# A transformer row kernel: 38 idle products of two columns ahead of TensorE's program in place of 6 of 128 columns

## Chip, cores and metric

The kernel runs on one core of a Trainium2 chip. The metric is the device time of one execution in microseconds, lower is better.

## The reference, cut to what matters

For each of 16 rows (batch entries) of 512 tokens by 512 features, in float32: a layer norm without gain or bias, `xn`; multi-head attention on `xn` with 16 heads of 32, causal mask, biases; a gated feed-forward on the same `xn`, with weights of -1, 0 or 1, 1408 wide, and scales per channel; the output is the sum of both and of the input.

```python
xn = _layernorm(x, axis=-1)
# attention
qkv = jnp.einsum('bsd,ed->bse', xn, w_qkv) + b_qkv
scores = jnp.einsum('bhqd,bhkd->bhqk', q, k) / math.sqrt(32) + causal
out = jnp.einsum('bhqk,bhkd->bhqd', softmax(scores), v) @ w_out.T + b_out
# feed-forward
g = (xn @ gate_w.T) * gate_s
u = (xn @ up_w.T) * up_s
ffn = ((silu(g) * u) @ down_w.T) * down_s
x + out + ffn
```

## The kernel before, in words

All large operands are split into two float16 parts, high and low, and a product in float32 precision is made of three float16 products (high by high, low by high, high by low). All weights stay in the core's memory for the whole run. Each engine has its own program, written out by hand, and they meet through semaphores alone.

**TensorE's program** (line 517 on) has four parts. First a lead-in: it waits for the constants (line 665), makes the idle products of `PE_PAD` (lines 666 to 668), turns the first maxima of the weights with `turn_max(0)` (line 669, defined at 643), spreads the scale with `spread(0)`, waits for the turned first row and computes q, k and v of row 0 (lines 672 to 683). Then `period(0, "first")`, a loop over rows 1 to 14 (lines 742 and 743), `period(B - 1, "last")` and `period(B, "tail")`. `period` has 20 slots. In every even slot it makes the scores of one unit of four heads (`scores`, line 605), in each slot a hand-written share (`PLAN`, line 66) of the products for q, k, v, gate, up, down and the output projection (`fill`, line 688), and the products of P by V of the slot two back (`values`, line 622), for which P has been turned by a DMA transpose that SP issues (lines 506 and 508). Every product goes through `mm` (line 519), so most of TensorE's work has line 520 in the profile. Products that write 512 columns take the bulk of the time; those of `values` write 68 or 34, those of the scores 128 to 512 on a quarter of the rows.

**The idle products** write `turned_max`, two partitions by 128 columns of bank 4, from the constants `ones` and `identity`. Nothing reads what they write: `turn_max(0)` starts the same place afresh. `turn_max(0)` waits for `qkv_batch`, which DVE raises once it has the maximum magnitude of the qkv weights in `amax` (line 959).

The hint at the loop's head is number 2,257, the branch back number 4,569, so the body has 2,313. It includes 26 short stretches under `pe.If` (lines 552 and 570), for low halves of the feed-forward weights; with weights of -1, 0 and 1 all low halves are zero, and these products are skipped.

**What orders the rest.** DVE takes the maxima of the scores and reads out results; ACT exponentiates and rounds to the high parts; POOL subtracts to get the low parts (line 1244 for P), normalises the next row (`normalise`, line 1220); SP issues every DMA in order: the transposes of P (lines 506, 508), of the next row's x (`turn_x`, line 439) in slot 15, of the attention output (`turn_o`, line 455), and loads and stores.

Of the kernel before, what the change touches and what calls it, by code (L numbers as in the profile page):

```python
# [40 lines left out]
CB = CW // P  # L41
LAG_V = 2

PE_PAD = 6

def regions(unit):
# [212 lines left out]
def block_program(nc, x, w_qkv, gate, up, w_out, down, smalls, b_out, down_s, out):  # L260
    with ExitStack() as ctx:
        def sb(name, shape, dt=F32):
            return ctx.enter_context(nc.sbuf_tensor(name, shape, dt))
# [29 lines left out]
        identity = sb("identity", [P, P])  # L293
        ones = sb("ones", [P, P])
# [38 lines left out]
        turned_max = ps[0:2, 4, 0:P]  # L333
# [184 lines left out]
        def _(pe):  # L518
# [145 lines left out]

            pe.wait_ge(consts_done, N_CONSTS)
            for _ in range(PE_PAD):
                nc.tensor.matmul(turned_max, lhsT=ones[:, 0:2], rhs=identity[:, :], start=True, stop=True,
                                 skip_group_check=True)
            turn_max(0)
            spread(0)  # L670
# [654 lines left out]
```

## Time and profile before

| | us |
|---|---|
| median of 3 runs | 1992.68 (1989.34 to 1994.12) |
| the profiled execution: its own time | 1988.57 |
| its span, first to last instruction | 1986.8 |
| matmuls busy (PE) | 1895.1, 95% of the span |
| weight loads busy (PEld) | 912.0, 46% |
| VectorE (DVE) | 1347.7, 68% |
| ScalarE (ACT) | 1295.6, 65% |
| GpSimd (POOL) | 1362.8, 69% |
| mean granted clock of TensorE | 0.989 of full speed |

Times are in microseconds from the start of the span unless marked ns. PE is TensorE's matmuls, PEld its weight loads, PEldq its sequencer's own instructions (branches, register work), DVE is VectorE, ACT ScalarE, POOL GpSimd, SP SyncE. A row names line, engine, operation, what is written and read, with shapes and count. Idle time of an engine is put down to what ended it; "issue" means that nothing the profile shows was waited for. A "busy" matmul isn't an array at its peak, since the ends are modelled. Queue 8 of the DMA listing, "instruction", carries program code.

### The profile page before, as it was taken

To read this page: it belongs to the slowest core of one execution; us is meant where nothing else is said; L and a number is where in the kernel's file an instruction comes from. 1 tells how busy PE (TensorE), PEld (TensorE's weight loads), DVE (VectorE), ACT (ScalarE), POOL (GpSimd) and SP (SyncE) were. 2 spreads that over 40 slices of the span, in tenths; PEclk is the share of its full clock that TensorE was granted. 3 is DMA by queue.
4 is the path that set the end of the run, shared out by engine and by line. 5 is a ranking of instruction groups with operands and counts; after the bars stand their busy time and mean duration, and the time that the engine had idled before them with its cause. 6 is when DMAs were issued, how large, how long until landed. Compare 5 with 4: busy or idle time off the path is not lost.

```text
span 1986.8 us, 48299 instructions
## 1 busy us (share of the span) xinstructions
PE 1895.1 (95%) x15560; PEld 912.0 (46%) x15560; DVE 1347.7 (68%) x3925; ACT 1295.6 (65%) x2315; POOL 1362.8 (69%) x1097
## 2 busy tenths in 40 slices
PE   5879999999999999999999999999999999999995
PEld 2334444444444444444444444444444444444442
DVE  7895666757667675666767566676766767666663
ACT  4776766766667666666766666676666766666662
POOL 1285786766768676686866768676676866768764
PEclk9889999999999999999999999999999999999998
DMA  9148768596776868768586776859677686876855
GB/s 333 38 83 152 145 112 153 106 158 133 120 144 120 144 128 149 144 113 154 104 157 128 139 147 110 151 112 157 138 121 144 116 148 128 149 144 114 154 86 117
DMA packets 840049, 267.89 MB, mean 135 GB/s; under 512 B 812864, under 2 KB 812864, under 8 KB 839232
## 3 DMA queue, kind: packets, MB, share of 16 engines
q1 hardware_dynamic: 839872, 265.15, 70.6%
q8 instruction: 158, 2.59, 0.6%
q14 instruction: 19, 0.16, 0.0%
HBM read 46.94 MB, written 16.78 MB: 32 GB/s over the span
## 4 chain that ended last, share of the span: by engine, by line
PE 59%; POOL 14%; issue 8%; DVE 7%; SPq 6%; DMA 4%; ACT 1%; DVEq 0%; POOLq 0%; ACTq 0%
PE ps L520 59%; POOL phl L1244 6%; SPq L442 4%; POOL region_b L1222 3%; DMA p_t<-phl 3%; POOL memory L1239 2%; DVE p L1155 2%; DVE memory L938 1%; SPq L508 1%; POOL region_a L1227 1%; SPq L506 1%; POOL rstd L1218 1%; DVE hidden_tmp L1069 1%; POOL o_hl L1249 1%; DVE hidden_tmp L1075 1%
## 5 line engine op out<-in xcount | busy, mean ns | idle before, releaser
L520 PE MATMUL ps<-x_t,memory 128*128 128x512 f16 x4384 | 1003.0, 381 | 16.3 <-DMA x_t<-region_a 6.7
L1244 POOL TENSOR_TENSOR phl<-p,phl 128x1024 f16<-128x1024 f32 x320 | 683.4, 2136 | 478.0 <-ACT phl L865 478.0
L855 ACT ACTIVATE p<-p,nmax 128x384 f32<-128x384 f32 (+3 forms) x1024 | 530.0, 557 | 288.3 <-DVE nmax L1155 268.9
L520 PEld LDWEIGHTS ps<-x_t,memory 128*128 128x128 f16 x4384 | 406.5, 98 | 513.7 <-issue 56.0
L1155 DVE CUSTOM_DVE_ANT_0 p<-ps,causal,cst 128x384 f32<-128x384 f32 (+3 forms) x1024 | 515.5, 547 | 98.3 <-PE ps L520 85.0
L865 ACT CAST phl<-p 128x1024 f16<-128x1024 f32 x320 | 334.1, 1044 | 52.4 <-DMA p_t<-phl 36.9
L520 PE MATMUL ps<-memory 128*128 128x512 f16 x1408 | 322.6, 379 | 0.8 <-DVE bout_bc L1007 0.8
L1239 POOL TENSOR_TENSOR memory<-hidden_tmp,memory 128x512 f16<-128x512 f32 x176 | 204.0, 1159 | 69.4 <-ACT memory L827 69.4
L1163 DVE TENSOR_REDUCE ps<-ps 128x132 f32<-128x264 f32 (+1 forms) x320 | 122.1, 381 | 184.3 <-PE ps L520 184.0
L520 PEld LDWEIGHTS ps<-vv,p_t 128*128 128x128 f16 x5120 | 187.3, 96 | 94.8 <-issue 21.3
L520 PE MATMUL ps<-vv,p_t 128*128 128x68 f16 (+1 forms) x5120 | 193.5, 185 | 16.1 <-DMA p_t<-phl 15.9
L520 PEld LDWEIGHTS ps<-memory 128*128 128x128 f16 x1408 | 131.4, 98 | 154.7 <-issue 6.6
L873 ACT CAST o_hl<-o 128x128 f16<-128x128 f32 (+1 forms) x320 | 87.8, 274 | 160.8 <-DVE o L1173 160.1
L520 PE MATMUL ps<-memory,region_a 128*128 128x512 f16 x768 | 175.3, 382 | 10.4 <-DMA region_a<-o_hl 10.4
L1069 DVE SCALAR_TENSOR_TENSOR hidden_tmp<-hidden_tmp,ps 128x512 f32<-128x512 f32 x176 | 120.1, 682 | 87.0 <-ACT hidden_tmp L820 86.5
L520 PE MATMUL ps<-memory,x_t 128*128 128x512 f16 x768 | 173.3, 379 | 0.0
L1025 DVE SCALAR_TENSOR_TENSOR qk<-ps,smalls_in,qk 128x512 f16<-128x512 f32 x128 | 96.0, 750 | 95.0 <-ACT qk L764 95.0
L820 ACT ACTIVATE hidden_tmp<-ps,tanh_scale 128x512 f32<-128x512 f32 x176 | 119.5, 679 | 51.8 <-PE ps L520 46.5
L520 PE MATMUL ps<-qk 32*128 32x128 f16 (+3 forms) x3072 | 135.8, 301 | 14.1 <-issue 9.1
L764 ACT ACTIVATE qk<-ps,smalls_in 128x512 f16<-128x512 f32 x128 | 87.3, 682 | 80.9 <-PE ps L520 79.1
L1249 POOL TENSOR_TENSOR o_hl<-o,o_hl 128x128 f16<-128x128 f32 (+1 forms) x320 | 126.1, 394 | 9.2 <-ACT o_hl L873 9.2
L1075 DVE SCALAR_TENSOR_TENSOR hidden_tmp<-hidden_tmp,h_scale,ps 128x512 f32<-128x512 f32 x176 | 130.8, 743 | 2.1
(78 smaller groups left out, 1320.1 us busy)
## 6 DMA issues: line engine op xcount, KB each, us to landing
region_b<-x SPq DMA_DIRECT2D x32, 1024.0 KB, 5.6
out<-region_b SPq DMA_DIRECT2D x64, 256.0 KB, 2.7
p_t<-phl SPq DMA_TRANSPOSE x640, 3.1
memory<-w_qkv SPq DMA_DIRECT2D x3, 1024.0 KB, 8.8
memory<-down SPq DMA_DIRECT2D x1, 2816.0 KB, 21.3
memory<-gate SPq DMA_DIRECT2D x1, 2560.0 KB, 9.5
memory<-up SPq DMA_DIRECT2D x1, 2560.0 KB, 15.3
x_t<-region_a SPq DMA_TRANSPOSE x64, 3.4
```

Of the source, the lines that this page charges most:

```text
L520: return nc.tensor.matmul(o, lhsT=l, rhs=r, start=start, stop=stop, skip_group_check=True)
L820: nc.scalar.activation(hidden_tmp[:, f % 2, :], ps[:, bank, :], ACT.Tanh, scale=tanh_scale[:, f:f + 1]).then_inc(sem["tanh_done"], 1)
L855: last = nc.scalar.activation(cols, cols, ACT.Exp, scale=-1.0, bias=nmax[:, s % 2, i:i + 1])
L865: nc.scalar.copy(phl[:, s % 2, 0, :], p32[:, s % 2, :]).then_inc(sem["p_hi"], 1)
L1025: v.scalar_tensor_tensor(out=qk[:, t, side, 1, :], in0=ps[:, bank, :], scalar=bqkv[:, tile:tile + 1], in1=qk[:, t, side, 0, :], op0=ALU.ad ...
L1069: v.scalar_tensor_tensor(out=hidden_tmp[:, f % 2, :], in0=hidden_tmp[:, f % 2, :], scalar=1.0, in1=ps[:, bank, :], op0=ALU.add, op1=ALU.mu ...
L1075: v.scalar_tensor_tensor(out=hidden_tmp[:, f % 2, :], in0=hidden_tmp[:, f % 2, :], scalar=h_scale[:, f:f + 1], in1=ps[:, bank, :], op0=ALU ...
L1155: v.tensor_tensor_reduce(p32[:, s % 2, col:col + w], ps[:, 2 * (s % 2) + jj, col - 512 * jj:col - 512 * jj + w], causal[:, S - w:S], cst[: ...
L1163: v.tensor_reduce(o_sums(n), o_halves(n), AX, ALU.add).then_inc(sem["o_sum"], 1)
L1239: g.tensor_tensor(h_t(1, f), hidden_tmp[:, f % 2, :], h_t(0, f), ALU.subtract)\
L1244: g.tensor_tensor(phl[:, s % 2, 1, :], p32[:, s % 2, :], phl[:, s % 2, 0, :], ALU.subtract)\
L1249: g.tensor_tensor(o_dst(s, 1), o_src(s), o_dst(s, 0), ALU.subtract).then_inc(sem["o_lo"], 1)
```

## The change

It raises the number of idle products in TensorE's lead-in from 6 to 38 and makes each write two columns instead of 128. They stand ahead of all else in TensorE's program, so everything behind them, the row loop included, moves back by the instructions added.

```diff
-PE_PAD = 6
+PE_PAD = 38
...
             pe.wait_ge(consts_done, N_CONSTS)
             for _ in range(PE_PAD):
-                nc.tensor.matmul(turned_max, lhsT=ones[:, 0:2], rhs=identity[:, :], start=True, stop=True,
+                nc.tensor.matmul(turned_max[:, 0:2], lhsT=ones[:, 0:2], rhs=identity[:, 0:2], start=True, stop=True,
                                  skip_group_check=True)
             turn_max(0)
             spread(0)
```

## Rows read from the trace of the kernel before

**Rows 1.** The page: busy times of the span, and the code's DMA queue.

```profile
PE 1895.1 (95%) x15560; PEld 912.0 (46%) x15560; DVE 1347.7 (68%) x3925; ACT 1295.6 (65%) x2315; POOL 1362.8 (69%) x1097
...
q8 instruction: 158, 2.59, 0.6%
```

**Rows 2.** Busy time in one iteration: length, then PE, PEld, DVE, ACT, POOL.

```profile
543.39:661.75 118.36, 116.61 (x968) 56.20 (x969) 79.74 (x241) 78.61 (x142) 85.45 (x69) 1.00 0.72 135
```

**Rows 3.** Waits of TensorE, whole span: us in total, times, longest.

```profile
PE ps L520 <- issue: 9.5, 14, 1.1
```

**Rows 4.** Waits of TensorE from 424.3 to 543.4, the same columns.

```profile
PE ps L520 <- DMA x_t<-region_a: 1.1, 1, 1.1
PE ps L520 <- DMA p_t<-phl: 0.5, 1, 0.5
```

**Rows 5.** Timeline of TensorE, first products of iterations: start, us, [idle before].

```profile
305.71 0.61 PE L520 MATMUL ps<-qk 32*128 32x512 f16 x8 [0.70 <-issue]
...
543.39 0.83 PE L520 MATMUL ps<-qk 32*128 32x512 f16 x12 [0.81 <-issue]
...
897.29 0.83 PE L520 MATMUL ps<-qk 32*128 32x512 f16 x12 [0.26 <-issue]
...
1723.70 0.83 PE L520 MATMUL ps<-qk 32*128 32x512 f16 x12 [0.50 <-issue]
```

**Rows 6.** Line 742, the loop: ns min/median/max, first and last start.

```profile
L742 PEldq COMPARE_BRANCH  x14: 85/1256/1624, 304.1 to 1839.6; - x14
```

**Rows 7.** The same line in two windows, around 541.7 and around 896.1.

```profile
L742 PEldq COMPARE_BRANCH  x1: 1304/1304/1304, 541.7 to 541.7; - x1
...
L742 PEldq COMPARE_BRANCH  x1: 806/806/806, 896.1 to 896.1; - x1
```

**Rows 8.** Timeline of TensorE where the loop is left.

```profile
1839.96 0.60 PE L520 MATMUL ps<-vv,p_t 128*128 128x68 f16 x16
1840.49 0.83 PE L520 MATMUL ps<-qk 32*128 32x512 f16 x12
```

**Rows 9.** DMA queues, 661.75 to 780.00, one iteration: packets, MB, share.

```profile
q8 instruction: 10, 0.16, 0.6%
```

**Rows 10.** DMA queues, in turn 540:541, 541:544, 544:545, 894:895.

```profile
q8 instruction: 1, 0.02, 6.0%
...
q1 hardware_dynamic: 1594, 0.40, 124.4%
...
q8 instruction: 1, 0.02, 5.5%
...
q8 instruction: 1, 0.02, 7.3%
```

**Rows 11.** Timeline of TensorE ahead of and behind one back edge.

```profile
534.18 2.76 PE L520 MATMUL ps<-x_t,memory 128*128 128x512 f16 x12
...
537.64 0.60 PE L520 MATMUL ps<-vv,p_t 128*128 128x68 f16 x16
538.09 4.04 PE L520 MATMUL ps<-memory 128*128 128x512 f16 x18
541.98 0.60 PE L520 MATMUL ps<-vv,p_t 128*128 128x68 f16 x16
...
548.06 3.18 PE L520 MATMUL ps<-memory,x_t 128*128 128x512 f16 x14
```

**Rows 12.** Timeline of TensorE, the idle products.

```profile
3.50 2.72 PE L667 MATMUL ps<-identity,ones 128*2 128x128 f32 x12 [3.50 <-POOL identity L1213]
```

**Rows 13.** The chain that ended last, its pieces on TensorE in one iteration.

```profile
543.39 61.48 PE ps L520 x508
...
660.67 1.08 issue
```

**Rows 14.** Timeline of TensorE, turn_max(0).

```profile
20.29 0.58 PE L646 MATMUL ps<-identity,amax 128*2 128x128 f32 x2 [14.07 <-DVE amax L959]
```

**Rows 15.** Timeline of TensorE, the first products of row 0.

```profile
26.62 6.74 PE L520 MATMUL ps<-x_t,memory 128*128 128x512 f16 x24 [4.19 <-DVE memory L938]
```

## The prediction, made before the changed kernel was run

> **What bounds the kernel now.** The page first: TensorE's array is busy for 95% of the span, the next engine for 69% [rows 1]. Within the steady row loop it is tighter: 116.61 of 118.36 us in one iteration [rows 2]. Whatever lets TensorE stand still there costs time, unless something else would have held it anyway. The whole idle time of the array, by what ended it, is short. Its one entry with no releaser is "issue", 9.5 us in 14 places [rows 3]; of the others, what recurs in the loop is a wait for turned x and one for turned P, 1.1 and 0.5 us in the iteration to 543.4 [rows 4].
>
> The timeline shows where those are. Thirteen stand before the first score products of an iteration, 0.26 to 1.08 us each, for example 0.81 before 543.39 and 0.26 before 897.29 [rows 5]; read at all thirteen back edges, from 305.71 to 1723.70, they add up to 9.11 us (the rest of the 9.5 is elsewhere). The line of the loop shows the cause: its closing COMPARE_BRANCH takes 1256 ns in the median [rows 6]. The same instruction took 1304 ns ahead of the idle 0.81 and 806 ahead of 0.26 [rows 5, 7]: the idle time is the branch less some 0.5 us that products already queued cover. The last of the loop's 14 branches, which leaves the loop and goes straight on, took 85 ns, the shortest of the fourteen [rows 6], and the array ran on without a gap from 1839.96 to 1840.49 [rows 8]. So what costs is going back, not the instruction.
>
> Why going back costs is read from the instruction queue. It moved 158 packets, 2.59 MB, or 16.4 KB each [rows 1]; an instruction of the compiled program has 64 bytes, so a packet is a block of 256. The loop body has 2,313 instructions, 9.04 blocks, and an iteration fetches ten [rows 9]: the body isn't kept, every block is fetched again, one at a time. Around the branch at 541.66 to 542.97 there is a packet in 540 to 541, none in 541 to 544 (that window has the data queue's alone), one in 544 to 545 [rows 10]. I read this as follows: on entering a block TensorE's sequencer asks for the next one, and in the block that holds the branch the hint at the loop's head makes that the head's block. The packet of 540 to 541 is the head's; the branch waits until it can be used; on landing the next block is asked for, and its packet follows 1.0 to 2.0 us after 542.97. The fetch is thus asked for 1.0 to 2.0 us before its packet and usable 2.0 to 3.0 us after that starts: 3.0 to 5.0 us in all, I take 4.
>
> How late the request is: 1.0 to 2.0 us ahead of 540 to 541 is 538.0 to 540.0, or 1.7 to 3.7 us before the branch. Products of 512 columns follow each other there at 0.22 us, two instructions each [rows 11], so the block with the branch is entered 16 to 34 instructions before it. Too late for a fetch of 4 us: 4 less 2.7 is the 1.3 us of the branch.
>
> **The change, part by part.**
> (a) Place. The six idle products are 12 weight loads and 12 matmuls in the records [rows 12], two of each per product. 32 more are 4 x 32 = 128 instructions, exactly half a block, ahead of everything. All block borders move back by 128 in the program. The branch then stands 144 to 162 instructions into its block, the head 136 to 154 (it is always 8 less, 2,312 being 9 x 256 + 8), and 154 + 2,313 = 2,467 is under 2,560: still ten blocks.
> (b) The branch. The head's block is asked for 128 instructions, some 61 products, earlier. Counting back from the branch: the 9 or so short products that remain of the sixteen, 18 long ones, 16 short, and 18 long of the stretch before (4, 12 and 2 more), from about 534 on: some 7 us earlier [rows 11]. With the 1.7 to 3.7 us of before the lead is about 9 us against at most 5.0 needed. The branch no longer waits for code, and the 0.5 us of queued products covers what is left of it (85 ns on leaving). Gain: the thirteen idles, 9.11 us. At the exit the next products even overlapped by 0.07 us (1839.96 + 0.60 against 1840.49) [rows 8], 13 x 0.07 = 0.9 more. Between 9.1 and 10.0 I take **9.5 us**.
> (c) Does it reach the end? The chain of one iteration runs from the products at 543.39 for 61.48 us, then over DVE to the normalisation of the next row, POOL's queue and SP's transposes back to the products of the last slots, and ends in 1.08 us of issue, the back edge itself [rows 13]. Array and chain both begin behind the edge, so each edge shortens the cycle by its own idle; the waits for x and P [rows 4] neither grow nor shrink. The bound from below is that half is swallowed, a gain of 4.6, where those transfers turn out to hang on something else; above, 10.0.
> (d) The new landing. From the head only 256 less 136 to 154, 102 to 120 instructions, are left to the next block, not some 240. It is asked for on landing, usable within 5.0 us. The timeline has 12, 16 and 16 products from the head to 548.06 [rows 5, 11], so the block begins 4 to 13 products after that, and the array needs it no earlier than 548.9 - 543.4 = 5.5 us after its first product. Cost 0; where the fetch took 2 us longer it would be 1 us an iteration at most.
> (e) The idle products themselves. Six of 128 columns took from 3.50 to 6.22 us, 2.72 for 12 records, about 0.21 apart [rows 12]. 76 at that pace, longer than two-column ones should need, end at 3.5 + 16.2 = 19.7 us. TensorE has nothing to do until DVE has the maxima of amax, which release turn_max(0) at 20.29 after 14.07 us of rest [rows 14]. Cost 0; the cover is 0.6 us, and past it each further 0.1 us would be paid once. They write only what turn_max(0) rewrites. A warmer array later is bounded by the first 24 products, 6.74 us against 24 x 0.22 = 5.3, a gain of at most 1.4 [rows 15]; with 6 us of rest still between, I take 0.
> (f) The exit. There the hint fetches a block that isn't used, and the one after it was only fetched some 5 us later. It is needed 128 instructions earlier now. Between 0 and one fetch, 5 us, once; the queue of products (the sequencer ran well over 16 products ahead) covers it, 0.
> No semaphore, DMA or other engine's instruction changes.
>
> Sum: 0 - 9.5 + 0 = -9.5 us on the profiled execution of 1988.57, giving 1979.1. That execution lies 4.1 under the median of the runs, 1992.68; on the median it is 1983.2.
>
> **Rivals.**
> R1, the place doesn't matter. The branch is taken to code that was last used ten blocks ago, so it fetches on demand wherever it stands, and the idle stays: 1992.7, within 0.3%. Against it: the packet comes before the branch, and the later the branch follows its packet the shorter it is (1304 ns with its packet 0.7 to 1.7 us ahead of 541.7, 806 with one of 894 to 895, 1.1 to 2.1 ahead of 896.1) [rows 7, 10]. The Trainium skill states such a rule (Runtime: NRT & Kernel Launch, Instruction fetch mechanics: a taken branch whose target isn't in the current two-page window forces a fetch before execution goes on); by it the 9.5 would be 0. The trace agrees that taken branches back cost 1256 ns and the fall-through 85, and doesn't show whether a hint is exempt. Chance 0.10.
> R2, the idle goes and comes back as waits for turned x or turned P, wholly or by half: a gain of 0 to 5 us, 1988 to 1993. For it: both waits are there in every iteration; against it: the chain crosses the edge. Chance 0.10.
> R3, slower. What made the exit's next packet so late may be a second request at mid-block, 128 instructions in. The branch now stands 16 to 34 behind that point, where it stood as far behind the border. Then the block after the loop is fetched just before going back, and if it takes the place of the head's block, or goes ahead of the one the landing needs, the branch waits for a whole fetch: 3.0 to 5.0 us, less 0.5 covered, against 0.70 now, so 1.8 to 3.8 more at 13 edges, 23 to 49 us: about 2029. It decides where only two blocks are held at a time. Against it: no eleventh packet is seen in an iteration. Chance 0.12.
>
> **How the numbers follow.** My case has 0.68, R1 and R2 0.10 each, R3 0.12. The measurement tells 0.3%, 6 us, from no change; my case gives 9.5, which clears that by 3.5, as much as runs differ. R2 and part of its neighbours stay under it. So faster 0.67, same 0.20, slower 0.13. The range leaves out R3 and the far end below: from 1979 (12 us gain with a low median, runs spread by 5) to 1993.5 (no gain). My case alone: 1979 to 1987.
>
> **What would show it.** Right: the loop's COMPARE_BRANCH under 400 ns at all 14, "issue" near 0 in the array's waits, ten instruction packets an iteration still, iterations of about 117.4 us, the turn of maxima still at 20.29. Wrong: branch as long as before with its packet still just ahead (the border isn't where I place it), branch longer or eleven packets (R3), branch short but the waits for x and P grown by the same 0.7 (R2), or the first products later than 26.62 (the idle products stick out).

## The result, and the profile after

The changed kernel takes 1970.1 us in the median (1969.0 to 1970.5, 4 runs) against 1992.1 us for the kernel before (1989.3 to 1994.1, 4 runs): a ratio of 0.9893, 95% interval 0.9878 to 0.9908. It is faster by 22 us, where 9.5 were forecast. The profiled executions are 1970.23 and 1988.57, 18.3 apart; the kernel before's lies some 4 us under its own median.

The page of the changed kernel: busy times, the code's queue, and the chain that ended last by engine.

```profile
span 1968.5 us, 48427 instructions
PE 1894.2 (96%) x15624; PEld 913.2 (46%) x15624; DVE 1347.6 (68%) x3925; ACT 1294.5 (66%) x2315; POOL 1361.9 (69%) x1097
...
q8 instruction: 158, 2.59, 0.6%
...
PE 80%; DVE 5%; POOL 5%; issue 4%; SPq 3%; DMA 2%; ACT 1%; DVEq 0%; POOLq 0%; ACTq 0%
```

The engines do the same work as in [rows 1], apart from the 64 records of the 32 added idle products. The chain that ended last now lies on TensorE for 80%, against 59% on the page of the kernel before. What the back edge costs is in the line of the loop and in the timeline around one edge (start, us, idle before):

```profile
L742 PEldq COMPARE_BRANCH  x14: 85/358/381, 304.9 to 1819.8; - x14
```

```profile
305.26 0.60 PE L520 MATMUL ps<-vv,p_t 128*128 128x68 f16 x16
305.80 0.83 PE L520 MATMUL ps<-qk 32*128 32x512 f16 x12
```

The branch fell from 1256 ns in the median [rows 6] to 358, and going back now looks like leaving the loop did in [rows 8]: the next products follow 0.06 us inside the modelled end of the last. The stretch from 304 to 1840 us holds 13 edges in either kernel. TensorE's waits in it, before:

```profile
PE ps L520 <- issue: 9.1, 13, 1.1
PE ps L520 <- DMA x_t<-region_a: 6.2, 10, 1.2
PE ps L520 <- DMA p_t<-phl: 4.4, 11, 0.5
```

and in the changed kernel, the whole answer:

```profile
PE ps L520 <- DMA p_t<-phl: 1.8, 5, 0.7
```

So 9.1 us of issue went, as forecast, and with them 8.8 of the 10.6 us of waits for turned x and turned P, which had been forecast to stay. Iterations are 116.2 to 117.1 us from edge to edge, against 117.3 to 119.1 before. Most of them have nothing left but products. Busy times of one iteration (length, then PE, PEld, DVE, ACT, POOL), to be held against [rows 2], and its instruction queue, as [rows 9]:

```profile
538.40:654.60 116.20, 116.20 (x974) 56.39 (x971) 79.51 (x239) 78.51 (x143) 85.11 (x69) 1.00 0.74 138
```

```profile
q8 instruction: 10, 0.16, 0.5%
```

The lead-in, in TensorE's timeline, against [rows 12, 14, 15]:

```profile
3.50 2.04 PE L667 MATMUL ps<-identity,ones 128*2 128x2 f32 x76 [3.50 <-POOL identity L1213]
20.66 0.59 PE L646 MATMUL ps<-identity,amax 128*2 128x128 f32 x2 [15.12 <-DVE amax L959]
...
27.00 8.02 PE L520 MATMUL ps<-x_t,memory 128*128 128x512 f16 x24 [4.20 <-DVE memory L938]
```

The 76 records take 2.04 us in all. The first products of row 0 begin 0.4 us later and take 1.3 us longer than before; both differ from kernel to kernel, one profiled execution each (26.62 to 27.12 and 6.62 to 8.02 among the kernels below, with no order by the number of idle products).

The account of the profiled pair goes by three stretches, cut at the first and the last start of the loop's branch. The lead-in got 0.8 us longer (304.1 to 304.9). The loop got 20.6 us shorter (1535.5 to 1514.9): 9.1 of issue, 13 x 0.06 of overlap at the edges and 8.8 of waits are 18.7 of it, and 1.9 stay unaccounted for. What comes behind the loop got 1.5 us longer (147.2 to 148.7). Together that is the 18.3.

### The profile page after: what moved, and what is told of

The parts are those of the page before. It is cut to its first block, busy times and chain, and to the rows that moved or that the text cites. A ratio compares the mean times of both kernels' runs of the same rounds, so it can differ in the third digit from the quotient of the medians.

```text
span 1968.5 us, 48427 instructions
## 1 busy us (share of the span) xinstructions
PE 1894.2 (96%) x15624; PEld 913.2 (46%) x15624; DVE 1347.6 (68%) x3925; ACT 1294.5 (66%) x2315; POOL 1361.9 (69%) x1097
## 4 chain that ended last, share of the span: by engine, by line
PE 80%; DVE 5%; POOL 5%; issue 4%; SPq 3%; DMA 2%; ACT 1%; DVEq 0%; POOLq 0%; ACTq 0%
PE ps L520 80%; POOL phl L1244 2%; DMA p_t<-phl 2%; SPq L442 1%; POOL region_b L1222 1%; DVE memory L938 1%; DVE p L1155 1%; POOL memory L1239 1%; SPq L506 1%; SPq L508 0%; POOL region_a L1227 0%; DVE hidden_tmp L1069 0%; SPq L456 0%; POOL rstd L1218 0%; DVE hidden_tmp L1075 0%
## 5 line engine op out<-in xcount | busy, mean ns | idle before, releaser
L820 ACT ACTIVATE hidden_tmp<-ps,tanh_scale 128x512 f32<-128x512 f32 x176 | 119.4, 679 | 51.3 <-PE ps L520 46.1
```

Of the source, the lines that this page charges most:

```text
L820: nc.scalar.activation(hidden_tmp[:, f % 2, :], ps[:, bank, :], ACT.Tanh, scale=tanh_scale[:, f:f + 1]).then_inc(sem["tanh_done"], 1)
```

## Experiments

Two explanations of the 8.8 us stood against each other. **S**: the stall at the edge itself delays the chain to x and P, more than the array. **P**: the change moved not only the branch but all ten code packets of an iteration, by half a block, and two of them had met SP's transposes ahead of x and P. All kernels were timed against the kernel before, taken again each time. The table has every one; shift is the number of instructions by which the loop stands later than in the kernel before, and the last two columns are TensorE's waits from 304 to 1840 us of the profiled execution.

| kernel | shift | ratio to before | issue, us | x and P, us |
|---|---|---|---|---|
| before | 0 | 1 | 9.1 | 10.6 |
| changed | 128 | 0.9893 | 0 | 1.8 |
| pad70 | 256 | 1.0000 (0.9991 to 1.0010) | 10.9 | 11.9 |
| pad2 | -16 | 0.9960 (0.9946 to 0.9975) | 15.5 | 0.9 |
| pad10 | 16 | 0.9996 (0.9987 to 1.0006) | 9.9 | 6.6 |
| pad14 | 32 | 0.9909 (0.9892 to 0.9925) | 0.2 | 4.3 |
| pad22 | 64 | 0.9913 (0.9897 to 0.9930) | 0 | 5.0 |
| pad30 | 96 | 0.9930 (0.9913 to 0.9946) | 0 | 8.9 |
| wide38 | 128 | 0.9884 (0.9868 to 0.9901) | 0 | 1.4 |
| pad46 | 160 | 0.9884 (0.9867 to 0.9900) | 0 | 3.2 |
| pad54 | 192 | 0.9929 (0.9912 to 0.9945) | 0.4 | 6.4 |
| nohint | 128 | 1.0175 (1.0158 to 1.0192) | 41.8 | 1.4 |
| skip_near | 0 | 0.9993 (0.9983 to 1.0002) | 9.4 | 11.3 |
| skip_far | 0 | 0.9948 (0.9932 to 0.9965) | 9.1 | 1.4 |

### Place or products: pad70

```diff
-PE_PAD = 38
+PE_PAD = 70
```

> 70 idle products of two columns: 256 instructions more than the kernel before, so the row loop stands at the same place within its block of 256, while more idle products are run than in the changed kernel. If only the place counts (both theories), this is the kernel before again: the closing branch at 1.0 to 1.6 us, issue idle of 9 us and waits for turned x and P of about 10 us in the loop, total 1990 to 1994. If the idle products themselves do something (for the array's state or the start), it is near 1970.

Measured 1991.4 us against 1991.2. A whole block further on, with 64 more idle products than it, the kernel is the kernel before again, branch and waits for x and P (11.9 us against 10.6, each in one execution) alike:

```profile
L742 PEldq COMPARE_BRANCH  x14: 85/1331/1721, 308.5 to 1847.5; - x14
```

So the idle products act through the place of what follows them, and through nothing else that these runs can tell (the interval is 0.1% wide on either side).

### Their width: wide38

The kernel before with `PE_PAD = 38`, products 128 columns wide.

> 38 idle products as in the changed kernel, but 128 columns wide as before: the same place of the loop, more work ahead of it. By the pace of 0.21 us for a pair of records they end at 19.7 us, ahead of turn_max(0) at 20.3, so the width is worth nothing: the same time as the changed kernel, 1969 to 1972. If the idle products' own work delays the start, it is longer by what they stick out.

Measured 1968.6 us, ratio 0.9884, the same as the changed kernel within the intervals. The products ended even earlier than bounded, 13.3 instead of 19.7 us:

```profile
3.51 9.81 PE L667 MATMUL ps<-identity,ones 128*2 128x128 f32 x76 [3.51 <-POOL identity L1213]
20.72 0.59 PE L646 MATMUL ps<-identity,amax 128*2 128x128 f32 x2 [7.40 <-DVE amax L959]
```

### Without the hint: nohint

```diff
-            with nc.Fori(1, B - 1, engines=type(mybir.ALL_ENGINES)([pe.engine]), hint_back_edge=True) as b:
+            with nc.Fori(1, B - 1, engines=type(mybir.ALL_ENGINES)([pe.engine]), hint_back_edge=False) as b:
```

> The changed kernel with hint_back_edge off in TensorE's loop alone: the branch must fetch its target on demand, about 3.5 to 4 us, idle some 3 us at each of 13 edges, 40 us in all, while the ten packets of an iteration keep their places apart from the one at the edge. Theory P: the waits for x and P stay near the 2 us of the changed kernel, total 2007 to 2012. Theory S: they come back at 10 us or more, total 2018 or more. If the hint has no effect (the rule that a taken branch fetches anyway), it is 1970.

Measured 2026.4 us, ratio 1.0175. The line of the loop, and the waits from 304 to 1840:

```profile
L742 PEldq COMPARE_BRANCH  x14: 76/3827/4107, 303.9 to 1877.3; - x14
```

```profile
PE ps L520 <- issue: 41.8, 13, 3.5
PE ps L520 <- DMA p_t<-phl: 1.4, 4, 0.6
```

The rival R1 falls: the hint does exempt the branch, which without it takes 3827 ns, the whole fetch (I had worked out 3.0 to 5.0). The packets say the same. Without the hint a packet still comes 5.9 to 7.3 us ahead of the branch, and an eleventh, which the changed kernel does without, starts 1.0 to 1.7 us behind the branch's own start. From the start of the packet that it waits for to its end the branch takes 2.3 to 2.9 us here, and 2.4 to 2.7 us at the thirteen edges of the kernel before: the same wait for the head's block, begun at different times.

And S loses its first test, though the total of 2026.4 us lies in the range that it was given (2018 or more): there are 3.2 us of stall at every edge, and no wait for x at all. Against P's range (2007 to 2012) the total is some 14 us too high, for a reason that neither theory had. Behind the long idle the granted clock fell to its lower level, 1.2 GHz, for a while. The timeline behind the first edge, and the window of it (the column before the last two is the granted clock):

```profile
308.25 1.47 PE L520 MATMUL ps<-qk 32*128 32x512 f16 x12 [3.47 <-issue]
309.64 5.74 PE L520 MATMUL ps<-memory,x_t 128*128 128x512 f16 x16
```

```profile
308.25:315.00 6.75, 6.75 (x27) 2.31 (x28) 1.43 (x4) 2.88 (x4) 1.65 (x1) 0.58 0.99 216
```

Twelve score products took 1.47 us where the changed kernel has 0.83, and the next sixteen 5.74, against 3.63 for sixteen at full clock. The clock fell behind nine of the thirteen edges, not behind the fifth to the eighth, though the idle there was as long (3.1 to 3.4 us):

```profile
796.00:803.00 7.00, 6.46 (x53) 3.10 (x54) 2.82 (x8) 2.92 (x4) 2.12 (x2) 1.00 0.84 159
```

The four iterations behind those edges took 119.4 to 119.9 us, which is the changed kernel's 116.5 and the 3.2 of stall; the others took 120.9 to 122.6. So the excess goes with the clock. Why it fell at some edges and not at others isn't shown.

### The packets moved, the edge left alone: skip_far and skip_near

Both are the kernel before, with two stretches in the loop body that never run. They stand behind a branch on the flag that is zero for these weights, 127 and 129 instructions long with it, 256 together. So the branch back stands as late in its block as before, and it takes as long (1156 and 1264 ns in the median of its thirteen jumps back, 1269 before). In skip_far they open slots 11 and 19, in skip_near slots 3 and 5; between the two the packets come half a block elsewhere.

```diff
+                def passed_over(n):
+                    with pe.If(has_lo["gate, up"] != 0):
+                        for _ in range(n):
+                            mm(ps[0:2, 4, 0:2], vv[:, 0, 0, 0:2], vv[:, 0, 0, 0:2], True, True)
+
                 for s in range(NCH if cur else TAIL_SLOTS):
+                    if mode == "mid" and s in (11, 19):
+                        passed_over({11: 63, 19: 64}[s])
```

> The kernel before, with two stretches of products in the loop body that are never run (passed over by a branch on the zero flag), 127 and 129 instructions long, at the start of slots 11 and 19. The branch back stands as late in its block as before (256 instructions more in the body), but between slots 11 and 19 the code packets come half a block elsewhere, away from the two places where they met SP's transposes before turned x and P. Theory P (packets meeting SP's transposes make x and P late): issue idle stays at 9 to 11 us, waits for x and P fall from 10.6 to 5 us or less, total 1983 to 1986. Theory S (the stall at the edge brings them on): all stays, 1991, or more for the eleventh packet.

> The same two passed-over stretches, but at the start of slots 3 and 5, so that only the packets of slots 3 and 4 move and those of the second half of an iteration lie where they lay in the kernel before. Both theories: the kernel before again, issue idle 9 to 11 us, waits for x and P about 10 us, total 1990 to 1994. If the stretches themselves cost something, it shows here and is to be taken off skip_far.

Measured: skip_far 1979.6 us against 1990.7, 11.1 faster; skip_near 1989.9 against the same, no difference that can be told. The waits, first of skip_far, then of skip_near:

```profile
PE ps L520 <- issue: 9.1, 13, 1.1
PE ps L520 <- DMA p_t<-phl: 1.4, 3, 0.6
```

```profile
PE ps L520 <- issue: 9.4, 13, 1.1
PE ps L520 <- DMA x_t<-region_a: 6.5, 10, 1.2
PE ps L520 <- DMA p_t<-phl: 4.8, 12, 0.5
```

This settles it between the two. With the same stall at the edge, and with the same two stretches to pass over, the waits for x and P are there or not by where the packets of the second half of an iteration fall: P holds, S falls. The total was expected at 1983 to 1986 and is lower, since nearly all of the 10.6 us went and not half. How a packet makes x and P late is seen on SP. The kernel before in one iteration (start, us), the instruction queue from 526.0 to 527.2, and the landing of the last of the four transposes of x, issued at 524.7 (min/median/max of that one):

```profile
517.54 2.52 SPq L508 DMA_TRANSPOSE p_t<-phl  x1
520.40 5.53 SPq L442 DMA_TRANSPOSE x_t<-region_a  x4
526.19 2.29 SPq L506 DMA_TRANSPOSE p_t<-phl  x1
528.59 1.24 SPq L508 DMA_TRANSPOSE p_t<-phl  x1
```

```profile
q8 instruction: 1, 0.02, 7.2%
```

```profile
DMA to landing us min/median/max: 4.9/4.9/4.9
```

The same of skip_far, where the last transpose of x is issued at 642.1; from 642 to 649 its DMA has the data queue alone and no code packet:

```profile
637.77 5.69 SPq L442 DMA_TRANSPOSE x_t<-region_a  x4
643.71 1.23 SPq L506 DMA_TRANSPOSE p_t<-phl  x1
645.06 1.27 SPq L508 DMA_TRANSPOSE p_t<-phl  x1
```

```profile
q1 hardware_dynamic: 5133, 1.28, 109.8%
```

```profile
DMA to landing us min/median/max: 3.5/3.5/3.5
```

A transpose takes SP 1.23 us to issue; these, where a code packet comes with it, 2.3 to 2.6 (that of 517.54, 93 us behind the head of 424.29, met the packet before, which falls between 518 and 519). And the last transpose of x, in flight when the packet comes, lands after 4.9 us instead of 3.4 or 3.5. Read over the whole loop of the kernel before, the 13 transposes of x that had a packet start between the end of their issue and their landing landed after 4.6 to 5.4 us, the other 39 after 3.3 to 4.2. The issue is less regular: of the 107 transposes that had a packet start between 0.6 us ahead of their own start and 0.9 us behind it, half took over 1.8 us and some the usual 1.23, and one transpose of P in every iteration took 2.4 to 3.4 us some 7 us behind the head, with no packet there. How a packet holds them up inside the DMA isn't shown. The one delay holds the products that need x (they began at 529.59, 524.7 + 4.9, after 1.15 us of waiting), the other the P of slot 15 behind it, which the products of slot 17 read, 0.52 us more. In skip_near the packet is back at this spot, and so is the slow issue:

```profile
644.70 1.23 SPq L506 DMA_TRANSPOSE p_t<-phl  x1
646.05 2.60 SPq L508 DMA_TRANSPOSE p_t<-phl  x1
```

The changed kernel has no packet there: its P transposes behind x take 1.23 and 1.26 us, and the last transpose of x, issued at 522.1, landed after 3.4. It has one earlier, within the four for x, which take 6.46 us together instead of 5.53 and still land in time.

```profile
516.90 6.46 SPq L442 DMA_TRANSPOSE x_t<-region_a  x4
523.61 1.23 SPq L506 DMA_TRANSPOSE p_t<-phl  x1
524.96 1.26 SPq L508 DMA_TRANSPOSE p_t<-phl  x1
```

### Other places: shifts of -16 to 192

Each is the changed kernel with another `PE_PAD`: 2, 10, 14, 22, 30, 46, 54.

> 10 idle products of two columns: the loop moves by 16 instructions only, so the head's block is asked for about 1.7 us earlier than in the kernel before, and the closing branch should take 0.4 us or less with no issue idle. The packets of code otherwise stay within about 2 us of where they were. Theory P (packets of code that fall on SP's transposes make turned x and P late, apart from the branch): the waits for x and P stay near 8 to 10 us in the loop, total about 1981 to 1984. Theory S (the stall at the edge itself brings those waits on): they go with it, total about 1970 to 1973.

Measured 1989.9 us: not as either theory said. The shift of 16 didn't free the branch (median 1342 ns, issue 9.9 us). The waits for x and P went down by 4 us all the same, without the stall having gone. The time didn't show it: the loop of the profiled execution is 3.5 us shorter than before (306.5 to 1838.5), but its lead-in is 2.4 us longer.

> 2 idle products of two columns, 16 instructions fewer than the kernel before. The loop's head then lies some 5 to 10 instructions ahead of a border, and so does the branch, or right at it. Landing there, the sequencer needs the next block at once and has only just asked for it: about 3.8 us (the fetch that the run without the hint showed), idle some 3 us at each of 13 edges, 40 us, whatever the branch itself takes; eleven packets an iteration. Total 2012 to 2030. If only the branch's distance from its border counted, the landing would cost nothing and the total be 1970 to 1995.

Measured 1983.8 us: a miss as well. There was no eleventh packet and no landing stall of 3 us. The branch took 1736 ns in the median and issue was 15.5 us, the most of all with the hint, while the waits for x and P were the smallest, 0.9:

```profile
PE ps L520 <- issue: 15.5, 13, 1.5
PE ps L520 <- DMA p_t<-phl: 0.9, 3, 0.4
```

Its P transposes behind x took 1.24 and 1.26 us. The largest stall goes with the smallest waits, once more against S.

> 14 idle products of two columns, 32 instructions more than before. The border of the branch's block now lies ahead of the wait at the start of the last values, so the head's block is asked for about 4 us before the branch: branch 0.35 to 0.5 us, issue idle at most 1 us. Theory P: the packet near 102 us stays close enough to SP's transposes to keep some 3 to 6 us of waits for x and P (as with 16 and 64 instructions), total 1974 to 1978. Theory S: as the changed kernel, 1970.

Measured 1972.0 us, branch 451 ns, issue 0.2, waits 4.3: 32 instructions are enough for the branch. The total is lower than I had set for such waits.

> 22 idle products of two columns: the loop moves by 64 instructions, the branch then has the head's block long before it is needed (0.35 us). Theory S: as the changed kernel, 1969 to 1973. Theory P: issue idle is gone, but the packets fall elsewhere between the transposes than at 0 or 128, so the waits for x and P come out between 2 and 10 us, total 1970 to 1982, not tied to the branch.

Measured 1973.5 us, branch 444 ns, waits of 5.0 us, all for P: inside what P gave, above what S gave.

> 30 idle products of two columns, 96 instructions more than before. No issue idle. Between 64 (waits for P of 5.0 us, 1973.5) and 128 (1.8 us, 1970.1), so the waits for x and P come out at 2 to 5 us: total 1970 to 1974.

Measured 1978.0 us, waits of 8.9 us, all for P: outside what I gave, and not between its neighbours. The trace shows why, and it is P once more at another spot. The waits stand at 91 us behind the head, not at 107, one in each iteration, and before them a packet now meets the transposes of the P that these products need. SP's issues, TensorE's wait, the queue from 863 to 864 and the landing of the transpose issued at 860.1:

```profile
860.11 1.24 SPq L508 DMA_TRANSPOSE p_t<-phl  x1
861.59 1.39 SPq L506 DMA_TRANSPOSE p_t<-phl  x1
```

```profile
865.09 0.62 PE L520 MATMUL ps<-vv,p_t 128*128 128x68 f16 x16 [0.72 <-DMA p_t<-phl]
```

```profile
q8 instruction: 1, 0.02, 5.9%
```

```profile
DMA to landing us min/median/max: 4.9/4.9/4.9
```

Over the thirteen iterations the same transpose lands after 4.8 to 5.0 us here, 4.4 to 4.9 in pad22 (which waits at this spot too, 5.0 us in all), 3.7 to 4.4 in the changed kernel and 3.1 to 3.3 in the kernel before.

> 46 idle products of two columns, 160 instructions more than before. No issue idle. Between 128 (1.8 us, 1970.1) and 192 (6.8 us, 1975.8): waits for x and P of 2 to 7 us, total 1970 to 1976.

Measured 1969.6 us, just under the range, waits 3.2. (The 6.8 us given for 192 counts the 0.4 of issue with them.)

> 54 idle products of two columns, 192 instructions more than before; the branch has its code 10 us ahead. Theory P: no issue idle, waits for x and P set by where the packets fall (about 84, 96 and 107 us after the head): one falls into SP's transposes of x, so 2 to 8 us, total 1971 to 1978. Theory S: as the changed kernel, 1970.

Measured 1975.8 us, waits 6.4, all for P, both as P gave. As P says, what is left once the branch is free isn't one value but goes up and down with the place, between 1.4 and 8.9 us. No place tried beats the changed kernel beyond the intervals; the best (0.9884 to 0.9893) can't be told apart.

## Why the prediction was right in part and wrong in its size

**The branch, steps (a) and (b): right.** It fell to 358 ns, issue went to nothing at all 13 edges, the iteration still fetches ten packets. The term was 9.5 us. The changed kernel against skip_far, which keeps the stall and has much the same waits for x and P (1.4 us against 1.8), gives 1979.6 - 1970.1 = 9.5 in absolute times, or 22.0 - 11.1 = 10.9 when each is set against its own runs of the kernel before.

**The step that failed is (c)**: "Array and chain both begin behind the edge, so each edge shortens the cycle by its own idle; the waits for x and P [rows 4] neither grow nor shrink". The first half stands. The second took it for granted that the chain to x and P is the same as before, since no instruction of SP changed. But the change moves the code packets, and these slow the transposes of SP that they meet: at 94 and 102 us behind the head of an iteration they had met the last transpose of P ahead of x, and the last of x. The term was put at nothing, and it was worth 8.8 us of waits here and 11.1 us of time in skip_far, more than the term that I had. Step (a) had said outright that all borders move by 128; what the packets themselves do to others I didn't price. The range went wrong with it: the most that the sum allowed was a gain of 10.0, because I counted one consequence of the place out of two. The rows that would have bounded it were there: the 1.1 and 0.5 us [rows 4] as a gain that could go, 10.6 us in the loop.

**The reading behind (b) is only partly right.** That the head's block is fetched shortly ahead of the branch and waited for is shown by nohint, by the branch's length at 0, 32 and 128, and by the 2.4 to 2.7 us from packet to branch's end. That the request comes on entering a block, 16 to 34 instructions ahead of the branch, isn't. That figure took the sequencer to read code at the pace of the products, 0.22 us for two instructions, so 16 instructions should have been 1.7 us. But the packet starts 0.8 to 1.8 us ahead of the branch at 0 and at 16 alike, 0.4 to 1.1 at -16, and 2.0 to 2.5 at 32. The expectation for pad14 put that down to the wait ahead of the last products of P by V, which lies between the two places; its numbers came true, but no run tests that wait by itself, and what triggers the request stays open.

**(d), the landing: right at the place of the change**, no wait behind any edge; at -16, where the model made it dear, the model failed. **(e): right**, cost 0, shown by wide38; the bound for the wide products was too high (their pace was 0.13 us a record, not 0.21). The sign of being wrong that was named, first products later than 26.62, did come, at 27.00, but not from the idle products: they ended at 5.54, and it was DVE that released `turn_max(0)` at 20.66 instead of 20.29. With 54 idle products the start is at 26.62 again. **(f), the exit: right**, nothing there to be seen.

**The rivals.** R1 fell by the changed kernel itself and by nohint. R2 had the right two waits and the wrong sign: they didn't take up the gain but added to it. Nor were both there in every iteration, as its argument said: x was waited for in 10 of 13, P in 11. R3, a second request at mid-block, didn't show: ten packets, and the branch fast at 128.

## What to carry to other kernels

Where a loop on TensorE is longer than what is kept of its code, its place in the program is a parameter with two effects: whether the block of the loop's head is there when the branch back comes, and which DMAs the code packets meet. Look at the length of the closing COMPARE_BRANCH and at the "issue" idle behind it for the first, and for the second at DMA-issuing instructions that take twice their usual time now and then; both can be moved at no cost that these runs show, by idle instructions ahead of the loop or by passed-over ones within it. When a change moves code, put the fetches on the list of what moves, beside instructions and DMAs, and give the waits near a bound resource a term in the sum, not only in the rivals.

## What the runs showed of the hardware that I had not expected

- A code packet of 16 KB can slow SP's issue of a DMA transpose from 1.23 us to between 2.3 and 2.6, and it slowed the landing of x in flight from 3.3 to 4.2 us to 4.6 to 5.4.
- A branch back without a hint took 3827 ns on TensorE, with a hint and code in time 344 to 381 ns, going straight on 76 to 93. Where it waits for its code, it ended 2.3 to 3.0 us after that packet's start, in every kernel here with the branch late.
- An idle of 3.47 us at an edge cost more than itself: a granted clock of 0.58 in the 6.75 us behind it, lower than full behind nine of thirteen such edges, and an iteration of 121.0 us ((1877.3 - 303.9) : 13) against 116.5, 4.5 us longer for 3.2 us of idle.
